# Causal attention in a two-layer block on one Trainium2 core: GpSimd inverts the row sums, VectorE masks four of the eight row blocks, and the order on all engines is new

## The chip, the cores and the metric

The kernel runs on one core of one Trainium2 chip. The metric is the device time of the program in microseconds (us): before, the median of three runs is 1507.27. The names in the profile are PE (TensorE, matrix products), PEld (its weight loads), DVE (VectorE), ACT (ScalarE), POOL (GpSimd) and SP (SyncE, which here issues all DMAs).

## The reference, cut to what matters

```python
# layer 0: x is (4, 1024, 128), 16 heads of 64
xn = layernorm(x)
qkv = einsum('bse,ehd->bshd', xn, qkv_w) + qkv_b
logits = einsum('bqhd,bkhd->bhqk', q, k) / sqrt(64)
logits = where(tril(ones(1024, 1024)), logits, large_negative)
probs = softmax(logits)
x = x + einsum('bhqk,bkhd->bqhd', probs, v) @ out_w + out_b + ffn(xn)   # ffn: silu(gate) * up
# layer 1, on the result: a delta-rule attention and a mixture of 8 experts; the change does not touch it
```

## The kernel before

Layer 0's attention is done in 32 units. Unit `u` is one batch (of 4) and one pair of heads (of 8). A unit has eight blocks of 128 query rows, called rows 0 to 7 here and in the code; row r sees keys 0 to 128(r+1). For each row and both heads:

1. TensorE makes the scores (L1022, `place_scores`) with q and k of 64 partitions for each head, so the two heads use one half each of the array's rows. Then it adds the triangular mask to the last 128 columns with one bf16 product for each head (L1024): identity times mask, accumulated on the scores.
2. VectorE takes the maximum, negated (`maximum`, L687). Rows 4 to 7 are done head by head, rows 0 to 3 both heads at once.
3. ScalarE takes the exponential (`softmax`, L528), which also gives the sum of the row, and writes into the buffer `big`.
4. VectorE takes the reciprocal of the row sums (`invert`, L697).
5. GpSimd multiplies the exponentials by it (`scale`, L447), head by head.
6. VectorE transposes 32 x 32 blocks in place (`turn`, L705).
7. When all rows of a group have been transposed, SP issues 16 DMAs (`move`, L354) that carry them from `big` to `across`, with the blocks exchanged between the partitions. Group 0 is rows 0, 1, 6, 7, group 1 is rows 2, 3, 4, 5.
8. One unit later TensorE multiplies them by the values (`weigh`, L1083), ScalarE copies the result (`keep_att`, L543), TensorE applies the output weights (`join`, L1107), ScalarE copies (`keep_join`) and GpSimd adds to `x1` (L459).

`big` has one place for each group. So the exponentials of a group in unit u+1 wait until its 16 DMAs of unit u have landed (the wait on `moved` in `softmax`), and so does `weigh` of unit u. The scores of rows 4 to 7 lie in `both`, those of rows 0 to 3 in `flips_all`, each with room for one row (rows 0 and 1 share), so the scores of the next row wait for the exponentials of the last.

Between these pieces, TensorE makes q, k and v of the next unit (`project`, L990; `project_values`, L1000), which ScalarE copies out (`keep_part`, `keep_values`). After each batch VectorE takes statistics of `x1` (`second_sums`, `second_variance` with L720), and one unit of the next batch has a `second_deviation` on GpSimd (L432 to L438). The order of every engine is written out by hand in its `unit(u)`; VectorE's `unit(u)` works on unit u-1. The `Tally` tables count semaphores in the same order.

Of the kernel before, what the change touches and what calls it, by code (L numbers as in the profile page):

```python
# [14 lines left out]
P = 128  # L15
# [74 lines left out]
TURNS = (5, 4)  # L90
SLOTS = [row for rows in STEP_ROWS for row in rows]
BANK = {('v', 0): 2, ('qk', 0, 1): 2, ('qk', 1, 0): 2, ('qk', 0, 0): 2, ('qk', 1, 1): 2, ('v', 1): 2, ('o', 0): 0, ('o', 1): 1}
# [30 lines left out]
EARLY = (('qk', 0, 1), ('qk', 1, 0))  # L123
# [39 lines left out]
def layer0(block, sem, sbuf, kept, early, shared, b2_sb, x, qkv_w, qkv_b, out_w, out_b, w_gate, w_up, w_down, ln_w, ln_b, w_slow, w_out, Wg, b1, late):  # L163
# [15 lines left out]
                ((7, 0), -1), ((7, 1), -1), ((0,), -1), ((1,), -1), ((6, 1), -1), ((6, 0), -1), ((2,), -1),  # L179
                ((5, 1), -1), ((5, 0), -1), ((3,), -1), ((4, 0), -1), ((4, 1), -1),  # L180
            ])
    exps_at = Tally([
                ((7, 0), 0), ((7, 1), 0), ((6, 1), 0), ((6, 0), 0), ((5, 1), 0), ((5, 0), 0), ((4, 0), 0),
                ((4, 1), 0),
# [8 lines left out]
                (('v', 0), 0), (('qk', 0, 1), 1), (('qk', 1, 0), 1), (('qk', 0, 0), 1), (('qk', 1, 1), 1),  # L193
                (('v', 1), 1),
# [5 lines left out]
                ((7, 1), 0), ((1, 1), 0), ((7, 0), 0), ((0, 0), 0), ((0, 1), 0), ((1, 0), 0), ((6, 0), 0),  # L200
                ((6, 1), 0), ((2, 0), 0), ((2, 1), 0), ((5, 0), 0), ((3, 0), 0), ((3, 1), 0), ((5, 1), 0),
# [3 lines left out]
                ((0,), -1), ((4,), -1), ((1,), -1), ((6,), -1), ((2,), -1), ((5,), -1), ((3,), -1),  # L205
# [7 lines left out]
    with ctx:  # L213
# [11 lines left out]
        recip = sb("recip", [P, 2, ROWS, 2])  # L225
        spare = sb("spare", [P, 1008])
# [22 lines left out]
        ident_made, mask_made, const_step, halves_made = sem("ident_made"), sem("mask_made"), sem("const_step"), sem("halves_made")  # L249
# [13 lines left out]
        recip_ready, scaled = sem("recip_ready"), sem("scaled")  # L263
        second_var, second_rstd, second_step, stats_step = sem("second_var"), sem("second_rstd"), sem("second_step"), sem("stats_step")
# [50 lines left out]
        def _(sp):  # L315
# [40 lines left out]
            for u in range(UNITS):  # L356
                if u == 2:
                    sp.wait_ge(xn_flipped, 2 * B)
                    sp.dma_start(w1_sb, W1.rearrange("x e h -> e x h")).then_inc(experts_loaded, 16)
                if u == UNITS - 1:  # L360
                    for c in range(2):
                        for half in range(2):
                            k, use = use_of(u, "qk", c, half)
                            sp.wait_ge(bank_made[k], use)
                    sp.dma_start(w2_sb, W2.rearrange("x (j p) e -> p x j e", p=P)).then_inc(experts_loaded, 16)
                    sp.wait_ge(b2_cleared, 1)
                    sp.dma_start(b2_sb[0:X, :], b2).then_inc(experts_loaded, 16)
                move(u, 0)
                move(u, 1)
# [3 lines left out]
        def _(pool):  # L373
# [47 lines left out]
            def constants():  # L421
# [5 lines left out]
                pool.memset(score[:], 0.0).then_inc(score_cleared, 1)  # L427

            def second_deviation(b):
# [9 lines left out]
                                   ALU.mult).then_inc(second_rstd, 1)  # L439

# [20 lines left out]
            def unit(u):  # L461
                scale(u, 7, 1)
                scale(u, 1, 1)
                scale(u, 7, 0)
                scale(u, 0, 0)
                scale(u, 0, 1)
                scale(u, 1, 0)
                scale(u, 6, 0)
                scale(u, 6, 1)
                scale(u, 2, 0)  # L470
                scale(u, 2, 1)
                if u > PAIRS and u % PAIRS == 2 and u < UNITS:
                    second_deviation(u // PAIRS - 1)
                scale(u, 5, 0)
                scale(u, 3, 0)
                scale(u, 3, 1)
                scale(u, 5, 1)
# [8 lines left out]
            tails["gpsimd"] = scale, add_part  # L486

        @block.scalar
        def _(act):
# [74 lines left out]
            def unit(u):  # L564
                if u == 0:
                    keep_values(0, 0)
# [4 lines left out]
                softmax(u, 0, 0)  # L571
                softmax(u, 0, 1)
                softmax(u, 1, 0)
                softmax(u, 1, 1)
                keep_part(u + 1, 0, 1)
                softmax(u, 6, 1)
                keep_part(u + 1, 1, 0)
                softmax(u, 6, 0)
                keep_att(u - 1, 0)
                keep_part(u + 1, 0, 0)  # L580
                softmax(u, 2, 1)
                softmax(u, 2, 0)
                softmax(u, 5, 1)
                softmax(u, 5, 0)
                softmax(u, 3, 1)
                softmax(u, 3, 0)
                keep_part(u + 1, 1, 1)
                keep_att(u - 1, 1)
                softmax(u, 4, 0)
                softmax(u, 4, 1)  # L590
                keep_values(u + 1, 1)
                keep_join(u - 1, 0)
                keep_join(u - 1, 1)
                keep_values(u + 1, 0)
# [58 lines left out]

# [5 lines left out]
        def _(dve):  # L659
# [13 lines left out]

            def maximum(u, row, *h):
# [4 lines left out]
                if step < SMALL:  # L679
                    dve.wait_ge(scores_ready, scores_at(u, step))  # L680
                else:
                    for k in h or range(2):
                        dve.wait_ge(bank_made[k], uses_at[k](u, "s", step))
# [4 lines left out]

            def invert(u, step):
                if done(u):  # L690
                    return
                recips_at.meet(u, step)
                for h in range(2):
                    dve.wait_ge(*exponents_of(u, step, h))
                lo = SLOTS.index(STEP_ROWS[step][0])
                part = slice(lo, lo + len(STEP_ROWS[step]))
                dve.reciprocal(recip[:, u % 2, part, :], row_sum[:, u % 2, part, :]).then_inc(recip_ready, 1)  # L697
# [33 lines left out]
            def unit(u):  # L731
                if u == 2:
                    constants()
                maximum(u - 1, 7, 0)
                maximum(u - 1, 7, 1)
                maximum(u - 1, 0)
                maximum(u - 1, 1)
                invert(u - 1, 0)
                invert(u - 1, 4)
# [6 lines left out]
                turn(u - 1, 7)  # L746
                turn(u - 1, 0)
                invert(u - 1, 1)
                maximum(u - 1, 2)
                turn(u - 1, 1)  # L750
                turn(u - 1, 6, 0)
                turn(u - 1, 6, 1)
                maximum(u - 1, 5, 1)
                invert(u - 1, 6)
                maximum(u - 1, 5, 0)
                if u == 1:
                    add_branch(B - 1, (1,))
                if batch_over(u - 3):
                    second_sums(u - 3, GROUPS[1])
                maximum(u - 1, 3)  # L760
                invert(u - 1, 2)
                turn(u - 1, 2)
                invert(u - 1, 5)
                maximum(u - 1, 4, 0)
                maximum(u - 1, 4, 1)
                if batch_over(u - 3):
                    second_variance(u - 3, GROUPS[0])
                turn(u - 1, 3)
                invert(u - 1, 3)
                turn(u - 1, 5)  # L770
                turn(u - 1, 4)
                if batch_over(u - 3):
# [88 lines left out]
            keep_part(0, 0, 1)  # L861
# [9 lines left out]
            keep_part(0, 1, 0)  # L871
# [5 lines left out]
            keep_part(0, 0, 0)  # L877
# [8 lines left out]
            tails["vector"] = maximum, invert, turn, second_sums, second_variance  # L886

        @block.tensor
        def _(pe):
# [124 lines left out]
            def place_scores(u, row):  # L1014

                q, k = qk_sb[:, u % 2, 0, :], qk_sb[:, u % 2, 1, :]
                lo, hi = place_of(row)
                for a in range(lo, hi, 512):
                    z = min(a + 512, hi)
                    for h in range(2):  # L1020
                        part = slice(D * h, D * (h + 1))
                        pe.matmul(scores_of(row, h)[:, a - lo:z - lo], lhsT=q[part, P * row:P * (row + 1)], rhs=k[part, a - lo:z - lo],  # L1022
                                  start=True, stop=z < hi)
# [87 lines left out]
            def unit(u):  # L1111
                if u == 0:
# [3 lines left out]
                project_values(u, 0)  # L1116
                score_small(u, 4)
                weigh(u - 1, 0, 0, 4)
# [3 lines left out]
                project(u + 1, 0, 1)  # L1122
                score_small(u, 6)
                project(u + 1, 1, 0)
                weigh(u - 1, 0, 4, 8)
                project(u + 1, 0, 0)
# [3 lines left out]
                project(u + 1, 1, 1)  # L1130
                score_small(u, 5)
                weigh(u - 1, 1, 0, 4)
                score(u, 3)
                weigh(u - 1, 1, 4, 6)
                project_values(u + 1, 1)
                join(u - 1, 0)
                join(u - 1, 1)
# [8 lines left out]
            project(0, 0, 1)  # L1146
# [8 lines left out]
            project(0, 1, 0)  # L1155
# [8 lines left out]
            project(0, 0, 0)  # L1164
# [7 lines left out]
            pe.wait_ge(v_loaded, 16)  # L1172
            project_values(0, 1)
            hidden(3, 2)

# [120 lines left out]
def layer1(block, sem, sbuf, kept, early, shared, ended, b2_sb, late, out):  # L1296
# [136 lines left out]
    with ctx:  # L1433
# [98 lines left out]
        def _(sp):  # L1532
            last_move = tails["sync"]
            for t in range(ROWS):
# [6 lines left out]
        def _(pool):  # L1541
# [80 lines left out]
            last_scale, last_add = tails["gpsimd"]  # L1622
# [573 lines left out]
        def _(dve):  # L2196
# [189 lines left out]
            last_maximum, last_invert, last_turn, last_sums, last_variance = tails["vector"]  # L2386
            last_maximum(UNITS - 1, 7, 0)
            last_maximum(UNITS - 1, 7, 1)
            last_maximum(UNITS - 1, 0)
            last_maximum(UNITS - 1, 1)  # L2390
            last_invert(UNITS - 1, 0)
            last_invert(UNITS - 1, 4)
            last_maximum(UNITS - 1, 6, 1)
            last_maximum(UNITS - 1, 6, 0)
            last_turn(UNITS - 1, 7)
            last_turn(UNITS - 1, 0)
            last_invert(UNITS - 1, 1)
            last_maximum(UNITS - 1, 2)
            last_turn(UNITS - 1, 1)
            last_turn(UNITS - 1, 6, 0)  # L2400
            last_turn(UNITS - 1, 6, 1)
            last_maximum(UNITS - 1, 5, 1)
            last_invert(UNITS - 1, 6)
# [876 lines left out]
```

## Time and profile before

| | |
|---|---|
| median of 3 runs | 1507.27 us (1505.23 to 1508.43) |
| profiled execution | 1510.43 us, with a span of 1508.7 us |
| mean TensorE clock granted | 0.99 of full speed |
| TensorE, VectorE, GpSimd, ScalarE busy | 97, 83, 64, 62% of the span |
| attention stage | about 95 to 957 us of the span |
| the chain that ended last | PE 62%, SP's DMA issues 13%, DVE 8%, DMA 5%, ACT 4% |

The shares are of the whole span, both layers together. The bulk of the time is a loop over the units with a constant pattern, so what a change of the loop is worth is read from one period and multiplied.

### The profile page before, as it was taken

The page shows a single profiled execution, that of the slowest core. Times are in us where ns is not written, and L with a number is a line of the kernel's source. Part 1 is how long each engine was busy: PE and PEld are TensorE (multiplying, and loading weights), DVE is VectorE, ACT ScalarE, POOL GpSimd, SP SyncE. Part 2 cuts the span into 40 slices and gives each one's busy share as a digit, 9 for nine tenths or more (in the row PEclk, how much of TensorE's full clock was granted, in tenths as well). Part 3 has the DMA queues.
Part 4 walks back from the last instruction along what each step waited for, and adds up shares of the span by engine and source line. Part 5 has one row for each costly group of instructions (what it writes and reads, how often), then busy time and mean ns, then how long its engine had stood idle before and what let it go on. Part 6 is the DMA issues. An engine that isn't in the chain of part 4 may idle for free.

```text
span 1508.7 us, 26195 instructions
## 1 busy us (share of the span) xinstructions
PE 1456.1 (97%) x8770; PEld 874.5 (58%) x8770; DVE 1252.7 (83%) x1966; ACT 928.3 (62%) x1862; POOL 967.3 (64%) x752
## 2 busy tenths in 40 slices
PE   8899999999999999999999999887999999999998
PEld 6645545555455455555554555454677676776767
DVE  7577787788777888877788778377999999999997
ACT  4356666666666666666666666444766676657562
POOL 5134555546545556455456554519999999999895
PEclk9989999999999999999999999998999999999999
DMA  8058777777777777778777778400000000000000
GB/s 186 1 126 200 169 169 180 179 163 174 180 169 174 168 181 173 166 172 184 167 171 169 184 173 191 107 1 1 1 8 7 1 8 1 8 8 1 8 1 15
DMA packets 77136, 163.91 MB, mean 109 GB/s; under 512 B 31410, under 2 KB 43724, under 8 KB 77004
## 3 DMA queue, kind: packets, MB, share of 16 engines
q1 hardware_dynamic: 77004, 162.24, 46.6%
q8 instruction: 72, 1.18, 0.3%
q14 instruction: 60, 0.49, 0.1%
HBM read 9.08 MB, written 2.10 MB: 7 GB/s over the span
## 4 chain that ended last, share of the span: by engine, by line
PE 62%; SPq 13%; DVE 8%; DMA 5%; issue 5%; ACT 4%; POOL 2%; DVEq 0%; ACTq 0%; POOLq 0%
SPq L354 13%; PE accum L1083 11%; PE both L2772 10%; PE both L1022 6%; PE flips_all L2795 5%; DVE big L705 5%; DMA across<-big 5%; PE flips_all L2784 4%; PE flips_all L1022 3%; ACT big L528 3%; PE flips_all L2832 3%; PE misc L990 2%; PE accum L2784 2%; PE accum L2795 2%; PE flips_all L2818 2%
## 5 line engine op out<-in xcount | busy, mean ns | idle before, releaser
L447 POOL TENSOR_SCALAR big<-big,recip 128x1024 f32<-128x1024 f32 (+7 forms) x512 | 374.4, 745 | 447.0 <-DVE recip L697 446.8
L705 DVE STREAM_TRANSPOSE big<-big 128x896 f32<-128x896 f32 (+7 forms) x288 | 345.5, 1226 | 4.7 <-POOL big L447 2.6
L687 DVE TENSOR_REDUCE neg_max<-both 128x1 f32<-128x1024 f32 (+3 forms) x256 | 249.7, 1007 | 73.8 <-PE both L1024 73.8
L1083 PE MATMUL accum<-across,v_sb 128*64 128x256 f32 (+1 forms) x2560 | 278.5, 364 | 0.0
L528 ACT ACTIVATE big<-both,neg_max 128x1024 f32<-128x1024 f32 (+3 forms) x256 | 242.8, 951 | 44.6 <-DVE neg_max L687 44.5
L1083 PEld LDWEIGHTS accum<-across,v_sb 128*64 128x64 f32 x2560 | 169.0, 137 | 100.0 <-issue 25.8
L1022 PE MATMUL both<-qk_sb 64*128 64x512 f32 (+3 forms) x1024 | 215.8, 540 | 5.7 <-ACT big L528 3.5
L2772 PE MATMUL both<-slow_sb,h_T 128*128 128x512 f32 x384 | 182.5, 602 | 10.8 <-DVE xnT L2285 7.2
L1581 POOL TENSOR_TENSOR prod<-xnT,qs 128x1024 f32<-128x1024 f32 (+3 forms) x32 | 180.1, 5636 | 0.0
L1022 PEld LDWEIGHTS both<-qk_sb 64*128 64x128 f32 x1024 | 89.0, 187 | 118.8 <-issue 115.1
L528 ACT ACTIVATE big<-flips_all,neg_max 128x128 f32<-128x128 f32 (+3 forms) x256 | 131.7, 525 | 41.0 <-DMA across<-big 29.0
L990 PE MATMUL misc<-xnT,w_qk 128*128 128x512 f32 x256 | 139.0, 625 | 0.8 <-ACT qk_sb L507 0.8
L507 ACT ACTIVATE qk_sb<-misc,columns 128x512 f32<-128x512 f32 x124 | 85.2, 687 | 78.2 <-PE misc L990 78.2
L2772 PEld LDWEIGHTS both<-slow_sb,h_T 128*128 128x128 f32 x384 | 70.4, 193 | 86.5 <-issue 68.4
L1022 PE MATMUL flips_all<-qk_sb 64*128 64x384 f32 (+3 forms) x512 | 103.7, 480 | 13.1 <-ACT big L528 12.7
L697 DVE RECIPROCAL recip<-row_sum 128x2 f32<-128x2 f32 (+1 forms) x224 | 36.4, 163 | 94.7 <-ACT big L528 94.7
L1573 POOL TENSOR_TENSOR prod<-xnT 128x1024 f32<-128x1024 f32 (+2 forms) x24 | 109.0, 4544 | 0.5 <-DVE misc L2319 0.3
L687 DVE TENSOR_REDUCE neg_max<-flips_all 128x2 f32<-128x256 f32 (+3 forms) x128 | 101.5, 812 | 5.0 <-PE flips_all L1024 4.4
L1619 POOL TENSOR_TENSOR terms<-terms 128x1024 f32<-128x1024 f32 x42 | 99.3, 2364 | 3.4 <-DVE terms L2373 1.4
L2795 PEld LDWEIGHTS flips_all<-w_qk,hid 128*128 128x128 f32 x736 | 87.0, 192 | 14.6 <-issue 9.4
L2325 DVE TENSOR_REDUCE misc<-prod 128x16 f32<-128x1024 f32 (+3 forms) x32 | 90.2, 2817 | 4.1 <-POOL prod L1581 4.0
L2795 PE MATMUL flips_all<-w_qk,hid 128*128 128x128 f32 x736 | 90.4, 276 | 1.3 <-ACT hid L1779 1.2
(223 smaller groups left out, 2381.2 us busy)
## 6 DMA issues: line engine op xcount, KB each, us to landing
across<-big SPq DMA_DIRECT2D x1024, 144.0 KB, 3.0
out<-x SPq DMA_DIRECT2D x8, 256.0 KB, 2.3
x<-in_L_attn_x SPq DMA_DIRECT2D x3, 512.0 KB, 5.7
slow_sb<-in_L_attn_w_slow SPq DMA_DIRECT2D x3, 512.0 KB, 7.7
w_qk<-in_L_attn_qkv_w SPq DMA_DIRECT2D x2, 512.0 KB, 6.4
xn<-in_L_ffn_W SPq DMA_DIRECT2D x1, 1024.0 KB
x<-in_L_attn_x SPq DMA_DIRECT2D x2, 256.0 KB, 2.9
qs<-in_L_attn_qkv_w SPq DMA_DIRECT2D x1, 512.0 KB, 6.1
```

Of the source, the lines that this page charges most:

```text
L354: sp.dma_start(across[g][32 * b:32 * (b + 1), a, :], runs[g][32 * a:32 * (a + 1), b, :]).then_inc(moved[g], 16)
L447: pool.tensor_scalar(part, part, recip[:, u % 2, SLOTS.index(row), h:h + 1], 0.0, ALU.mult, ALU.add).then_inc(scaled, 1)
L528: last = act.activation(probs_of(row, h).rearrange("p b j k -> p j b k"), scores_of(row, h).rearrange("p (j b k) -> p j b k", b=MOVES, k=3 ...
L687: dve.tensor_reduce(out=dst, in_=src, axis=AX.X, op=ALU.max, negate=True).then_inc(max_ready, 1)
L705: dve.transpose(part, part).then_inc(turned[group_of(row)], 1)
L990: pe.matmul(pool_of[k], lhsT=w_qk[:, c, P * n:P * (n + 1)], rhs=xnT[:, u // PAIRS, 512 * half:512 * (half + 1)], start=True, stop=True).th ...
L1022: pe.matmul(scores_of(row, h)[:, a - lo:z - lo], lhsT=q[part, P * row:P * (row + 1)], rhs=k[part, a - lo:z - lo], start=True, stop=z < hi)
L1083: last = pe.matmul(dst, lhsT=values_of(u, j, h), rhs=keys_of(g, rows[n:n + 2], j, h), start=j == 0, stop=j == rows[n + 1])
L1573: pool.tensor_tensor(prod[s % 2][:, 0:s, :], ks[:, 0:s, :], ks[:, s:s + 1, :].broadcast_to([P, s, HD]), ALU.mult).then_inc(prod_ready, 1)
L1581: pool.tensor_tensor(prod[s % 2][:, s:2 * s + 1, :], ks[:, 0:s + 1, :], qs[:, s % 2:s % 2 + 1, :].broadcast_to([P, s + 1, HD]), ALU.mult). ...
L2772: last = pe.matmul(places[k][:, 512 * half:512 * (half + 1)], lhsT=h_T[:, P * s:P * (s + 1)], rhs=slow_sb[:, c, 512 * half:512 * (half + 1 ...
L2795: last = pe.matmul(places[k][:, P * s:P * (s + 1)], lhsT=hid[:, e % 2, j, P * s:P * (s + 1)], rhs=w2_sb[:, e, j, :], start=j == 0, stop=j ...
```

## The change

GpSimd takes over `invert`: the row sums to the power minus one, as a two-tensor instruction with a constant tile `minus_one`. VectorE loses its reciprocals and gets `cover`, which adds the mask to the last 128 columns of the scores of rows 0 and 1 (together), 2 and 3, in PSUM, ahead of their maximum. TensorE loses the mask products of these four rows and keeps those of rows 4 to 7. Every engine has a new order.

```diff
+COVERED = (4, 5, 6)          # the steps of rows (0, 1), 3 and 2
...
+            def invert(u, step):     # gpsimd
+                if done(u):
+                    return
+                recips_at.meet(u, step)
+                for h in range(2):
+                    pool.wait_ge(*exponents_of(u, step, h))
+                lo = SLOTS.index(STEP_ROWS[step][0])
+                part = slice(lo, lo + len(STEP_ROWS[step]))
+                pool.tensor_tensor(recip[:, u % 2, part, :], row_sum[:, u % 2, part, :], minus_one[:, 0:len(STEP_ROWS[step]), :], ALU.pow).then_inc(recip_ready, 1)
...
+            def cover(u, step):      # vector
+                if done(u):
+                    return
+                covers_at.meet(u, step)
+                scored(u, step, range(2))
+                rows = STEP_ROWS[step]
+                if len(rows) == 1:
+                    lo, hi = place_of(rows[0])
+                    part, wide = (both if step < SMALL else flips_all)[:, :, hi - P:hi], mask.unsqueeze(1)
+                else:
+                    part = flips_all[:].rearrange("p h (r k) -> p h r k", r=2)[:, :, :, 0:P]
+                    wide = mask.unsqueeze(1).unsqueeze(1)
+                dve.tensor_tensor(part, part, wide.broadcast_to(part.shape), ALU.add).then_inc(covered, 1)
...
-                dve.reciprocal(recip[:, u % 2, part, :], row_sum[:, u % 2, part, :]).then_inc(recip_ready, 1)
...
             def unit(u):             # tensor
+                project(u + 1, 1, 0)
...
                 score(u, 0)
-                project_values(u, 0)
                 score_small(u, 4)
+                project_values(u + 1, 0)
...
             def place_scores(u, row):
...
+                if step_of(row) in COVERED:
+                    return last
                 return [pe.matmul(scores_of(row, h)[:, P * row:P * (row + 1)], lhsT=ident_half[:], rhs=mask_half[:],
                                   start=False, stop=True) for h in range(2)]
```

On TensorE, in the second half of a unit. Before, the rows are the scores of row 5, a projection, row 3, the weighing of group 1 (key blocks 0 to 3), row 4:

```order
L1022 MATMUL both<-qk_sb 128x512 x2
L1022 MATMUL both<-qk_sb 128x256 x2
L1024 MATMUL both<-mask_half,ident_half 128x128 x2
L990 MATMUL misc<-xnT,w_qk 128x512
L1022 MATMUL flips_all<-qk_sb 128x512 x2
L1024 MATMUL flips_all<-mask_half,ident_half 128x128 x2
L1083 MATMUL accum<-across,v_sb 64x4x64 x6
L1083 MATMUL accum<-across,v_sb 64x4x32 x2
L1083 MATMUL accum<-across,v_sb 64x4x64 x8
L1022 MATMUL both<-qk_sb 128x512 x2
L1022 MATMUL both<-qk_sb 128x128 x2
L1024 MATMUL both<-mask_half,ident_half 128x128 x2
```

And of the change, in the same place (its lines have other numbers; L1052 is the scores, L1056 the mask, L1115 the weighing):

```order
L1052 MATMUL both<-qk_sb 128x512 x2
L1052 MATMUL both<-qk_sb 128x256 x2
L1056 MATMUL both<-mask_half,ident_half 128x128 x2
L1029 MATMUL misc<-qs,xnT 128x256 x2
L1115 MATMUL accum<-across,v_sb 64x4x64 x6
L1115 MATMUL accum<-across,v_sb 64x4x32 x2
L1115 MATMUL accum<-across,v_sb 64x4x64 x8
L1052 MATMUL flips_all<-qk_sb 128x512 x2
L1115 MATMUL accum<-across,v_sb 64x4x64 x2
L1115 MATMUL accum<-across,v_sb 64x4x32 x2
L1052 MATMUL both<-qk_sb 128x512 x2
L1052 MATMUL both<-qk_sb 128x128 x2
```

The first weighing now stands in front of row 3's scores, and the second (key blocks 4 and 5) in front of row 4's.

On VectorE, from the maxima of row 5 to the end of the unit. Before:

```order
L687 TENSOR_REDUCE neg_max<-both 128x1
L697 RECIPROCAL recip<-row_sum 128x2
L687 TENSOR_REDUCE neg_max<-both 128x1
L687 TENSOR_REDUCE neg_max<-flips_all 128x2
L697 RECIPROCAL recip<-row_sum 128x2
L705 STREAM_TRANSPOSE big<-big 128x4x192
L697 RECIPROCAL recip<-row_sum 128x2
L687 TENSOR_REDUCE neg_max<-both 128x1 x2
L705 STREAM_TRANSPOSE big<-big 128x4x256
L697 RECIPROCAL recip<-row_sum 128x2
L705 STREAM_TRANSPOSE big<-big 128x4x384
L705 STREAM_TRANSPOSE big<-big 128x4x320
```

And of the change (L717 is the mask's addition):

```order
L730 TENSOR_REDUCE neg_max<-both 128x1 x2
L717 TENSOR_TENSOR flips_all<-flips_all,e_buf 128x2x128
L730 TENSOR_REDUCE neg_max<-flips_all 128x2
L730 TENSOR_REDUCE neg_max<-both 128x1 x2
L738 STREAM_TRANSPOSE big<-big 128x4x384
L738 STREAM_TRANSPOSE big<-big 128x4x192
L738 STREAM_TRANSPOSE big<-big 128x4x256
L738 STREAM_TRANSPOSE big<-big 128x4x320
```

The transposes of rows 5, 2, 3 and 4 now all stand behind the maxima of row 4; before, row 2's stood in front of them.

On GpSimd, the same part of the unit, in the change alone (before, these are the same scalings without L457, with row 3's two between row 5's):

```order
L457 TENSOR_TENSOR recip<-row_sum,minus_one 128x2
L465 TENSOR_SCALAR big<-big,recip 128x4x3x32 x2
L457 TENSOR_TENSOR recip<-row_sum,minus_one 128x2
L465 TENSOR_SCALAR big<-big,recip 128x4x6x32 x2
L457 TENSOR_TENSOR recip<-row_sum,minus_one 128x2
L465 TENSOR_SCALAR big<-big,recip 128x4x4x32 x2
L457 TENSOR_TENSOR recip<-row_sum,minus_one 128x2
L465 TENSOR_SCALAR big<-big,recip 128x4x5x32 x2
```

A power now stands in front of each row's two scalings.

## Rows read from the trace of the kernel before

**Rows 1.** Page, part 1: busy time of the engines and share of the span.
```profile
PE 1456.1 (97%) x8770; PEld 874.5 (58%) x8770; DVE 1252.7 (83%) x1966; ACT 928.3 (62%) x1862; POOL 967.3 (64%) x752
```

**Rows 2.** Chain that ended last, 395 to 423: start us, us, what.
```profile
395.12 0.80 PE accum L1083 x8
...
401.82 0.42 PE flips_all L1022 x4
...
402.45 0.63 PE flips_all L1022 x4
...
415.99 1.09 PE flips_all L1022 x4
417.08 0.22 PE flips_all L1024 x2
417.30 3.39 PE accum L1083 x32
420.69 1.28 PE both L1022 x8
...
422.19 0.82 PE accum L1083 x8
```

**Rows 3.** Timeline of VectorE, 414 to 429: start us, us, what [idle before].
```profile
413.97 2.06 DVE L705 STREAM_TRANSPOSE big<-big 128x896 f32<-128x896 f32 x2
...
422.23 1.55 DVE L687 TENSOR_REDUCE neg_max<-both 128x1 f32<-128x640 f32 x2 [1.62 <-PE both L1024]
423.70 1.24 DVE L705 STREAM_TRANSPOSE big<-big 128x1024 f32<-128x1024 f32 x1
425.38 0.17 DVE L697 RECIPROCAL recip<-row_sum 128x2 f32<-128x2 f32 x1 [0.44 <-ACT big L528]
425.48 3.35 DVE L705 STREAM_TRANSPOSE big<-big 128x1536 f32<-128x1536 f32 x2
```

**Rows 4.** Timeline of ScalarE, 402 to 425.
```profile
402.89 1.11 ACT L528 ACTIVATE big<-both,neg_max 128x1024 f32<-128x1024 f32 x1 [0.44 <-DVE neg_max L687]
...
414.62 0.58 ACT L528 ACTIVATE big<-flips_all,neg_max 128x384 f32<-128x384 f32 x1 [0.53 <-DMA across<-big]
...
423.62 0.79 ACT L528 ACTIVATE big<-both,neg_max 128x640 f32<-128x640 f32 x1
```

**Rows 5.** Timeline of GpSimd, 412 to 428.
```profile
412.65 2.00 POOL L447 TENSOR_SCALAR big<-big,recip 128x896 f32<-128x896 f32 x2 [2.72 <-DVE recip L697]
...
425.64 1.57 POOL L447 TENSOR_SCALAR big<-big,recip 128x640 f32<-128x640 f32 x2 [2.70 <-DVE recip L697]
```

**Rows 6.** Timeline of VectorE: last two transposes of units 1 and 30.
```profile
124.14 3.35 DVE L705 STREAM_TRANSPOSE big<-big 128x1536 f32<-128x1536 f32 x2
...
920.41 3.35 DVE L705 STREAM_TRANSPOSE big<-big 128x1536 f32<-128x1536 f32 x2
```

**Rows 7.** VectorE in 260 to 1040, shapes apart: busy us, mean ns.
```profile
L687 DVE TENSOR_REDUCE neg_max<-flips_all 128x2 f32<-128x1024 f32 x25 | 30.3, 1213 | 2.6 <-PE flips_all L1024 2.6
...
L2285 DVE SCALAR_TENSOR_TENSOR qs<-both,e_buf 128x1024 f32<-128x1024 f32 x4 | 4.9, 1222 | 5.6 <-ACT e_buf L1835 5.6
...
L720 DVE BATCH_NORM_AGGREGATE var<-stats 128x2 f32<-128x6 f32 x32 | 2.9, 152 | 0.1
```

**Rows 8.** GpSimd in 0 to 260, shapes apart.
```profile
L447 POOL TENSOR_SCALAR big<-big,recip 128x512 f32<-128x512 f32 x14 | 9.5, 692 | 4.8 <-DVE recip L697 4.8
...
L401 POOL TENSOR_TENSOR e_buf<-e_buf,minus_half 128x8 f32<-128x8 f32 x3 | 5.1, 1696 | 0.2
...
L394 POOL TENSOR_TENSOR e_buf<-e_buf,minus_half 128x4 f32<-128x4 f32 x2 | 2.0, 1014 | 0.2
```

**Rows 9.** Timeline of GpSimd, 582 to 593.
```profile
582.70 0.20 POOL L432 TENSOR_TENSOR rstd<-var,eps 128x8 f32<-128x8 f32 x1
...
586.79 3.13 POOL L447 TENSOR_SCALAR big<-big,recip 128x768 f32<-128x768 f32 x4
590.52 1.57 POOL L447 TENSOR_SCALAR big<-big,recip 128x640 f32<-128x640 f32 x2 [0.61 <-DVE recip L697]
```

More of the change, by code:

```diff
@@ L367, in _ @@
                     sp.dma_start(b2_sb[0:X, :], b2).then_inc(experts_loaded, 16)
+                move(u - 1, 1)
                 move(u, 0)
-                move(u, 1)
             tails["sync"] = move
@@ L652, in _ @@
             silu(3, 2)
+            keep_part(0, 0, 0)
             for u in range(UNITS):
@@ L678, in maximum @@
                 step = step_of(row)
[L679 to L683, printed above, removed]
+                scored(u, step, h or range(2))
+                if step in COVERED:
+                    dve.wait_ge(covered, covers_at(u, step))
                 src, dst = both_scores(row), neg_max[:, u % 2, row, :]
@@ L733, in unit @@
                     constants()
-                maximum(u - 1, 7, 0)
-                maximum(u - 1, 7, 1)
+                cover(u - 1, 4)
                 maximum(u - 1, 0)
                 maximum(u - 1, 1)
-                invert(u - 1, 0)
-                invert(u - 1, 4)
                 maximum(u - 1, 6, 1)
@@ L746, in unit @@
                 turn(u - 1, 7)
+                cover(u - 1, 6)
+                turn(u - 1, 1)
+                maximum(u - 1, 2)
                 turn(u - 1, 0)
-                invert(u - 1, 1)
-                maximum(u - 1, 2)
-                turn(u - 1, 1)
+                turn(u - 1, 6, 1)
                 turn(u - 1, 6, 0)
-                turn(u - 1, 6, 1)
+                maximum(u - 1, 5, 0)
                 maximum(u - 1, 5, 1)
-                invert(u - 1, 6)
-                maximum(u - 1, 5, 0)
                 if u == 1:
@@ L759, in unit @@
                     second_sums(u - 3, GROUPS[1])
+                cover(u - 1, 5)
                 maximum(u - 1, 3)
[L761 to L763 removed]
+                maximum(u - 1, 4, 1)
                 maximum(u - 1, 4, 0)
[L765 removed]
                 if batch_over(u - 3):
                     second_variance(u - 3, GROUPS[0])
+                turn(u - 1, 5)
+                turn(u - 1, 2)
                 turn(u - 1, 3)
[L769 to L770 removed]
                 turn(u - 1, 4)
+                maximum(u, 7, 0)
+                maximum(u, 7, 1)
                 if batch_over(u - 3):
@@ L885, in _ @@
                 unit(u)
-            tails["vector"] = maximum, invert, turn, second_sums, second_variance
+            tails["vector"] = cover, maximum, turn, second_sums, second_variance
         @block.tensor
@@ L1017, in place_scores @@
                 lo, hi = place_of(row)
+                last = [None, None]
                 for a in range(lo, hi, 512):
@@ L1021, in place_scores @@
                         part = slice(D * h, D * (h + 1))
-                        pe.matmul(scores_of(row, h)[:, a - lo:z - lo], lhsT=q[part, P * row:P * (row + 1)], rhs=k[part, a - lo:z - lo],
-                                  start=True, stop=z < hi)
+                        last[h] = pe.matmul(scores_of(row, h)[:, a - lo:z - lo], lhsT=q[part, P * row:P * (row + 1)], rhs=k[part, a - lo:z - lo],
+                                  start=True, stop=z < hi or step_of(row) in COVERED)
+                if step_of(row) in COVERED:
+                    return last
                 return [pe.matmul(scores_of(row, h)[:, P * row:P * (row + 1)], lhsT=ident_half[:], rhs=mask_half[:],
```

159 lines of the change are left out of this document (82 added, 77 removed).

## The prediction

> **What bounds the kernel now.** The page's first part [rows 1] shows TensorE 97% busy, VectorE 83%, GpSimd 64%. That suggests that work taken from TensorE is gained in full. The chain that ended last says otherwise: 13% of it are SP's DMA issues. So I looked for a loop that the moves close, and read the timelines of the unit at 402 to 429.
>
> The loop runs through group 1. Row 2's exponential starts at 414.62, and the idle time before it was ended by a DMA [rows 4]. The unit's last two transposes start at 425.48 and take 3.35, so they end at 428.83 [rows 3]: 14.21 later. Then SP issues the 16 DMAs of group 1, they land, and row 2's next exponential starts. One period is (920.41 - 124.14)/29 = 27.46 over units 1 to 30 [rows 6], so the move takes 27.46 - 14.21 = 13.25 on average. TensorE needs nearly as much: in the chain the weighing at 395.12 and the one at 422.19 are the same place of two units, 27.07 apart, with nothing but TensorE between them [rows 2]. The reader is to see two limits 0.4 apart: the move loop at 27.46, which rules, and TensorE at 27.07.
>
> **TensorE after the change.** A row's mask products take 0.22 [rows 2], so four rows give 0.88. There is more. The scores of row 0 (128 columns, 0.42) and row 1 (256 columns, 0.63) differ by 0.21 for 128 columns, so each carries 0.21 that does not depend on its columns [rows 2]: the price of coming from the full array to two halves. Row 1 now follows row 0, and row 5 follows row 2, directly: 0.42 less. Two products that stood behind a cheap mask product now come straight from the halves: I charge 0.15 each (bounds 0 and 0.21). TensorE's need falls to 27.07 - 0.88 - 0.42 + 0.3 = 26.07.
>
> **The move loop after the change**, counted from row 2's exponential as 0.
> - TensorE: weighing of group 1 starts at 0.14 (it waits for the same DMAs), 3.39, then row 3's scores 1.09 [rows 2]: 4.62. Weighing of blocks 4 and 5: 0.82 + 0.15. Row 4: 1.28 + 0.22 [rows 2]. Row 4 is ready at 7.1; before it was 422.19 - 414.62 = 7.57.
> - VectorE: its first maximum starts 0.04 later, 7.13. The two take 1.47 (422.23 to 423.70), row 3's transpose 1.16 (1.24 less the 0.08 that neighbours overlap), those of rows 5 and 4 3.35 together [rows 3], less 0.1 since they are apart. Row 2's is 0.9, by the line through 1.07 for 896 elements (half of 2.06, and overlap) and 1.24 for 1024 [rows 3]. The last would start at 7.13 + 1.47 + 1.7 + 0.9 + 1.16 = 12.4 and end at 13.9.
> - The power. No row has one of two elements. 128x4 takes 1.01 and 128x8 1.70 [rows 8], 0.17 an element; the line gives 0.67 for 128x2. Lower bound: the reciprocal's 0.17 [rows 3]; upper bound: 1.01. I take 0.67, since the line has its two ends near it.
> - The mask's addition. Two tensors, one in PSUM, 1024 elements: 1.22; the smallest VectorE row here 0.15 [rows 7]. 256 elements by the line: 0.42 (bounds 0.15 and 1.22). Row 3: ready 4.62, masked 5.08, maximum 1.21 [rows 7] to 6.36. That is before row 4 is ready, with 0.77 to spare, so VectorE's additions are hidden while they take less than 1.2. The two other additions stand where VectorE waits for row 6 and where it waits for the move.
> - GpSimd: row 3's exponentials follow at 6.38. Row 4's pair takes 1.76 with the hop to the next engine (423.62 to 425.38) [rows 3, 4]; 512 columns instead of 640 take 0.1 less each, so 7.93. Power 0.67; hop 0.07; two scalings of 0.69 [rows 8] less overlap, 1.35; power 0.67; hop 0.07; two scalings of row 4, 1.57 [rows 5]; hop 0.1. That makes 12.43, a hair behind VectorE's 12.4. Row 4's transpose 1.52 ends the loop at 13.95.
>
> So two things meet: TensorE delivers row 4 0.47 earlier; row 2's transpose, which now stands behind row 4's maxima, and the powers take that back but for 14.21 - 13.95 = 0.26. The period is 27.20, still the move loop's. TensorE, at 26.07, then waits over 1 us in each period.
>
> [...] By the rows the power costs four times the reciprocal (0.67 against 0.17). [...]
>
> **Terms that take back.**
> - In three units GpSimd computes the deviations, 582.70 to 586.79, 4.1 us [rows 9]. Before, this was hidden: GpSimd idled 0.61 in front of row 4's scalings [rows 9]. Now four powers are in the same queue. From row 2's exponentials at 1.2: 0.77, 0.6, 4.1, 0.6, 0.67, 1.8, 0.67, 1.35, 0.67, 0.07 + 1.57, 0.1 and 1.52 make 15.8, which is 1.85 over 13.95: 3 x 1.85 = 5.5.
> - In three units the four aggregates of 0.15 [rows 7] now stand between row 4's maxima and the transposes, in the loop: 3 x 0.5 = 1.5.
> - Group 0 has a loop too: from row 7's exponential, 402.89, to its last transpose, 413.97 + 2.06 = 416.03 [rows 3, 4], is 13.14; with the move 26.4. GpSimd there gets powers of 1.01 and 0.67 in front of scalings that ended 1.38 ahead of the last transpose (414.65 [rows 5]), about one transpose ahead, so with little slack. I expect 0.6 to 1.2 more: 27.0 to 27.6, around the new period. Moves vary, so part of this shows: 0.05 in 30 periods, 1.5.
> - The first unit has no move ahead of it and gains from TensorE: -0.5. Layer 1 keeps its instructions, and the chain that leads into it is the same.
>
> **Sum.** 30 x -0.26 + 5.5 + 1.5 + 1.5 - 0.5 = +0.2. On the profiled execution's 1510.4 that is 1510.6; on the median, 3.1 below it, 1507.5. Each 0.1 us in the loop is 3 us.
>
> **The rivals.**
> - The full gain of TensorE. 27.46 to 26.07 in 31 units, 43 us less or 1464. For it: TensorE 97% busy. Against: row 2's exponential is released by a DMA [rows 4], and what the loop computes between two moves, 13.95, is fixed by waits in which TensorE's gain is only partly contained. Chance 0.05.
> - A shorter loop. Power under 0.6 (VectorE's 13.9 rules), deviations cost 1 us a unit, group 0 nothing: 30 x -0.31 + 3 + 1.5 - 0.5 = -5, so 1502; with TensorE's products closer, down to 1496. Chance 0.32.
> - The power as the bound. With power p the loop ends at 12.61 + 2p; from p = 0.73 on it is over 14.07, at which the other terms make it slower than before by the bound below. At 0.85 it ends at 14.31: +3 and the 8 us of the other terms and 1.5 for the deviations, 1520; at 1.01, 14.63, 1531. For it: the smallest power in the trace is 1.01. Chance 0.2.
> - Group 0's loop rules, at 27.6: 30 x 0.14 + 5.5 + 1.5 - 0.5 = +11, 1518. It decides from 1.0 us more between row 7's exponential and the last transpose of group 0. Chance 0.13.
> - My forecast, no change within 0.2%: 0.3.
>
> **How the numbers follow.** A measurement of this kernel can tell about 0.2% (3 us) from no change. Faster: 0.05 + 0.32 = 0.37. Same: 0.3. Slower: 0.2 + 0.13 = 0.33. Both signs hold much, so the forecast's own range is 1504.5 to 1510.5, and the range for 8 in 10 reaches from 1496 to 1521: it leaves out the full gain and the dearest powers.
>
> **What would show it.** In the profile after: TensorE's share falls by 2 to 4 points with a wait in front of the weighing of group 1; row 2's exponential still released by a DMA; 13.9 to 14.0 from it to the end of row 4's transpose; powers of 0.67; additions of 0.42 to 0.5; the period 27.2; units with deviations over 1 us longer. The prediction is wrong if row 2's exponential waits for no DMA any more, if the powers are far from 0.67, or if GpSimd is what row 6's transposes wait for in every unit.

## The result and the profile after

The changed kernel takes 1514.69 us (median of 10 runs, 1512.58 to 1519.84) against 1507.27 for the kernel before (median of 10 as well): ratio 1.005 (95% interval 1.0038 to 1.0061). It is slower by 0.5%, inside the range and on its upper side, not the 1507.5 forecast. The profiled execution took 1519.84, the slowest of the ten, and has a span of 1518.1, 9.4 over the 1508.7 before. Below, the 9.4 are divided by loop and unit; they are differences of two single executions.

The page's first part answers [rows 1]:

```profile
PE 1428.7 (94%) x8514; PEld 876.2 (58%) x8514; DVE 1273.0 (84%) x1838; ACT 921.1 (61%) x1862; POOL 1132.8 (75%) x977
```

TensorE does 27 us less and 256 matmuls less, and the kernel is longer. GpSimd does 166 us more, which is what its powers take: six of 0.70 and one of 1.01 in each of 32 units, 167.

The ordinary unit. These are the changed kernel's timelines of ScalarE, of VectorE and of GpSimd in one unit (start us, us, what, idle before and releaser); they answer [rows 3, 4, 5].

```profile
393.39 0.58 ACT L553 ACTIVATE big<-flips_all,neg_max 128x384 f32<-128x384 f32 x1 [2.03 <-DMA across<-big]
...
399.89 0.69 ACT L553 ACTIVATE big<-flips_all,neg_max 128x512 f32<-128x512 f32 x1 [0.43 <-DVE neg_max L730]
```

```profile
398.06 0.43 DVE L717 TENSOR_TENSOR flips_all<-flips_all,e_buf 128x256 f32<-128x256 f32 x1 [1.32 <-PE flips_all L1052]
398.63 1.22 DVE L730 TENSOR_REDUCE neg_max<-flips_all 128x2 f32<-128x1024 f32 x1
400.25 1.55 DVE L730 TENSOR_REDUCE neg_max<-both 128x1 f32<-128x640 f32 x2 [0.40 <-PE both L1056]
401.73 3.75 DVE L738 STREAM_TRANSPOSE big<-big 128x1536 f32<-128x1536 f32 x3
406.09 1.51 DVE L738 STREAM_TRANSPOSE big<-big 128x1280 f32<-128x1280 f32 x1 [0.61 <-POOL big L465]
```

```profile
398.73 1.79 POOL L465 TENSOR_SCALAR big<-big,recip 128x768 f32<-128x768 f32 x2
401.48 0.70 POOL L457 TENSOR_TENSOR recip<-row_sum,minus_one 128x2 f32<-128x2 f32 x1 [0.96 <-ACT big L553]
402.28 1.37 POOL L465 TENSOR_SCALAR big<-big,recip 128x512 f32<-128x512 f32 x2
403.61 0.70 POOL L457 TENSOR_TENSOR recip<-row_sum,minus_one 128x2 f32<-128x2 f32 x1
404.41 1.58 POOL L465 TENSOR_SCALAR big<-big,recip 128x640 f32<-128x640 f32 x2
```

Row 2's exponential is still released by a DMA. From its start to the end of row 4's transpose it is 406.09 + 1.51 - 393.39 = 14.21, the same as before, and 14.19 to 14.21 in all but eight units. The other three transposes are done at 401.73 + 3.75 = 405.48, and the last waits 0.61 for GpSimd. So GpSimd ends the loop, not VectorE: mask addition, maximum, exponentials, two powers and four scalings follow each other.

A period is counted here from the end of one unit's row 4 transpose to the next. What varies in it is the move, from that end to the next row 2 exponential: it takes 12.82 to 14.21 behind units 2 to 29 (12.80 to 14.11 before). SP starts its 16 issues 0.03 after the transpose and needs 10.1 to 11.6 for them, most of them 0.64 apart. So most of the move is the issuing of 16 DMAs; no experiment here changed it.

Two things are not ordinary. In unit 2 the chain that ended last (start us, us, what) reads:

```profile
136.98 0.92 PE misc L1029 x4
137.90 4.46 issue
142.36 6.08 PE accum L1115 x32
```

TensorE idles 4.46, then the 32 products of the first weighing, 3.39 in [rows 2], take 6.08. The reason for the idle stands on ScalarE:

```profile
142.35 0.58 ACT L553 ACTIVATE big<-flips_all,neg_max 128x384 f32<-128x384 f32 x1 [6.13 <-DMA across<-big]
```

And in the order of SP's queue. Here are the kernel before and the changed kernel, in the same stretch:

```profile
104.71 33.41 SPq L354 DMA_DIRECT2D across<-big  x38
138.16 0.58 SPq L359 DMA_DIRECT2D xn<-in_L_ffn_W  x1
141.80 3.71 SPq L354 DMA_DIRECT2D across<-big  x6
```

```profile
104.74 18.73 SPq L360 DMA_DIRECT2D across<-big  x20
123.51 0.68 SPq L365 DMA_DIRECT2D xn<-in_L_ffn_W  x1
125.40 20.11 SPq L360 DMA_DIRECT2D across<-big  x25
```

The new order of SP issues layer 1's 1 MB of W1 between the moves of group 0 and group 1 of unit 1; before, it stood behind group 1's move. Group 1 of unit 1 then moves in 17.0 us instead of 13.5. The table of busy times (length, each engine's busy us, TensorE's clock as a share of full, DMA share, GB/s) shows why the weighing is then slow:

```profile
120.00:137.00 17.00, 17.00 (x103) 8.72 (x102) 14.34 (x15) 11.28 (x26) 12.56 (x17) 1.00 0.99 237
137.00:142.30 5.30, 0.90 (x4) 0.44 (x3) 4.60 (x6) 0.00 (x0) 1.74 (x2) 0.87 0.69 163
142.30:148.50 6.20, 6.14 (x34) 3.95 (x36) 0.00 (x0) 3.49 (x9) 4.30 (x6) 0.56 0.91 218
148.50:157.00 8.50, 8.00 (x46) 4.49 (x48) 6.83 (x7) 5.93 (x13) 3.75 (x6) 1.00 0.42 87
```

The clock granted is 0.56 while the weighing runs, so most of it ran at the 1.2 GHz level, after 4.46 of idleness; it is 1.00 from 148.5 on. Unit 2's period is 33.80 against 27.67 before: +6.1 of the 9.4, in one unit.

The other thing is the unit with deviations. GpSimd of the changed kernel, unit 10:

```profile
366.65 0.59 POOL L465 TENSOR_SCALAR big<-big,recip 128x384 f32<-128x384 f32 x1
367.20 0.20 POOL L440 TENSOR_TENSOR rstd<-var,eps 128x8 f32<-128x8 f32 x1
...
371.29 0.59 POOL L465 TENSOR_SCALAR big<-big,recip 128x384 f32<-128x384 f32 x1
...
377.32 1.58 POOL L465 TENSOR_SCALAR big<-big,recip 128x640 f32<-128x640 f32 x2
```

The deviations stand between row 2's two scalings and delay all that follows. The loop of these three units (10, 18 and 26) is 16.04 or 16.05; before, it was 14.51, 14.55 and 14.20, so 4.9 are added. Six units (these and the one ahead of each) take 171.20 against 164.51: +6.7. The units ahead have loops of 14.20 and are 2.1 longer for longer moves.

The rest: first unit -1.2, unit 1 -0.9, the other 22 periods of 3 to 30 together -1.25; together with the two above 6.1 + 6.7 - 1.2 - 0.9 - 1.25 = 9.45. The last unit's period is 31.20 instead of 28.94, +2.3, which what follows it gives back.

### The profile page after: what moved, and what is told of

Same layout as the page of the kernel before. It is cut to its first block, busy times and chain, and to the rows that moved or that the text cites. A ratio compares the mean times of both kernels' runs of the same rounds, so it can differ in the third digit from the quotient of the medians.

```text
span 1518.1 us, 25876 instructions
## 1 busy us (share of the span) xinstructions
PE 1428.7 (94%) x8514; PEld 876.2 (58%) x8514; DVE 1273.0 (84%) x1838; ACT 921.1 (61%) x1862; POOL 1132.8 (75%) x977
## 4 chain that ended last, share of the span: by engine, by line
PE 76%; DVE 8%; issue 6%; POOL 5%; ACT 2%; SPq 2%; DMA 1%; DVEq 0%; ACTq 0%; POOLq 0%
PE accum L1115 14%; PE both L2799 10%; PE both L1052 9%; PE misc L1019 7%; PE flips_all L1052 5%; PE flips_all L2822 5%; PE flips_all L2811 4%; PE misc L1029 3%; PE flips_all L1139 3%; DVE neg_max L730 3%; PE flips_all L2859 3%; PE accum L2811 2%; POOL big L465 2%; PE accum L2822 2%; SPq L360 2%
## 5 line engine op out<-in xcount | busy, mean ns | idle before, releaser
L465 POOL TENSOR_SCALAR big<-big,recip 128x384 f32<-128x384 f32 (+7 forms) x512 | 375.9, 749 | 22.1
L457 POOL TENSOR_TENSOR recip<-row_sum,minus_one 128x2 f32<-128x2 f32 (+1 forms) x224 | 166.7, 744 | 270.6 <-ACT big L553 270.6
L1115 PE MATMUL accum<-across,v_sb 128*64 128x256 f32 (+1 forms) x2560 | 282.3, 368 | 27.9 <-issue 27.9
L1115 PEld LDWEIGHTS accum<-across,v_sb 128*64 128x64 f32 x2560 | 182.4, 139 | 154.5 <-issue 95.8
L1052 PE MATMUL both<-qk_sb 64*128 64x512 f32 (+3 forms) x1024 | 211.1, 530 | 11.1 <-ACT big L553 10.6
L1052 PEld LDWEIGHTS both<-qk_sb 64*128 64x128 f32 x1024 | 93.4, 187 | 123.2 <-issue 123.1
L717 DVE TENSOR_TENSOR flips_all<-flips_all,e_buf 128x256 f32<-128x256 f32 (+1 forms) x96 | 49.5, 516 | 66.9 <-PE flips_all L1052 66.9
L1052 PE MATMUL flips_all<-qk_sb 64*128 64x384 f32 (+3 forms) x512 | 95.1, 469 | 0.0
```

The source lines that it names most:

```text
L457: pool.tensor_tensor(recip[:, u % 2, part, :], row_sum[:, u % 2, part, :], minus_one[:, 0:len(STEP_ROWS[step]), :], ALU.pow).then_inc(reci ...
L465: pool.tensor_scalar(part, part, recip[:, u % 2, SLOTS.index(row), h:h + 1], 0.0, ALU.mult, ALU.add).then_inc(scaled, 1)
L1052: last[h] = pe.matmul(scores_of(row, h)[:, a - lo:z - lo], lhsT=q[part, P * row:P * (row + 1)], rhs=k[part, a - lo:z - lo], start=True, st ...
L1115: last = pe.matmul(dst, lhsT=values_of(u, j, h), rhs=keys_of(g, rows[n:n + 2], j, h), start=j == 0, stop=j == rows[n + 1])
```

## The experiments

Four theories, in the letters of the expectations: A, W1's load ahead of a move costs some 5 us; C, the deviations between row 2's scalings cost some 5; E, GpSimd's powers end the ordinary loop and take back what TensorE lost; H, the power alone costs what the loop's arithmetic gives for it. All ratios are to the kernel before on the same chip (medians 1508.06 to 1508.28), with the 95% interval. Between the kernel before of the result, 1507.27, and these lies 0.8 to 1.0; a difference of two medians is uncertain by that much at least.

**W1's load back behind the move, in the changed kernel.**

```diff
-                if u == 2: (wait, W1's dma_start)
                 move(u - 1, 1)
+                if u == 2: (wait, W1's dma_start)
```

> The changed kernel with one edit: the 1 MB load of W1 is issued behind the 16 DMAs of group 1 of unit 1, where the kernel before has it, and not in front of them. Theory A (the load's place costs some 6 us: row 2's exponential of unit 2 waits 4.1 us longer than usual, TensorE idles and then runs one weighing at 0.56 of its clock): 1507.5 to 1509, period of unit 2 back from 33.8 to about 27.5. Rival B (unit 2 is slow because the new order needs a unit to settle): 1514 to 1515.5, no change.

1510.89, ratio 1.002 (1.0007 to 1.0033); the changed kernel had 1.005. Unit 2's period is 28.40 and its loop 14.19. The chain shows what is left:

```profile
138.87 1.69 issue
140.56 3.46 PE accum L1115 x32
```

After an idle of 1.69 the weighing keeps its 3.46. The time is above A's range and far from B's. A's mechanism holds, its price was too high: 33.80 - 28.40 = 5.4 in unit 2 of the profiles, 3.8 between the medians (4.8, if each is taken against its own kernel before). The profile of the change shows a dear case: in the four other traces of the experiments with the load in the same place and SP's new order, unit 2 takes 30.89 to 31.87.

**The same load between the moves, in the kernel before.**

> The kernel before with one edit: the load of W1 is issued between the DMAs of group 0 and of group 1 of unit 1, as in the changed kernel. Theory A: 1510 to 1514, a period of some 33 at unit 2 and a clock near half in its first weighing. Rival B: 1506.5 to 1508, no change.

1511.47, 1.002 (1.0007 to 1.0032). Unit 2's period is 31.57 and its weighing takes 5.03:

```profile
144.60 1.13 PE flips_all L1022 x4
145.73 0.22 PE flips_all L1024 x2
145.94 5.03 PE accum L1083 x32
```

The clock granted is 0.68 in that weighing. One line moved on SP costs some 3 us in a kernel with nothing else changed. A holds from the other side; the price is smaller here than the 3.8 (1514.69 - 1510.89) there, by less than these runs tell apart.

**Deviations behind row 4's scalings, in the changed kernel.**

```diff
-                if u > PAIRS and ...: second_deviation(u // PAIRS - 1)
                 scale(u, 4, 0)
                 scale(u, 4, 1)
+                if u > PAIRS and ...: second_deviation(u // PAIRS - 1)
```

> The changed kernel with one edit: the deviations of the second norm (4.1 us on GpSimd in three units) stand behind the scalings of row 4, not between those of row 2. Theory C (in the GpSimd queue of the new kernel they push row 4's scalings and so the last transpose): 1509 to 1511, periods of units 10, 18, 26 from 29.0 to about 27.3. Rival D (these units are long because of VectorE's statistics and aggregates, which are in them or next to them): 1513.5 to 1515.

1512.03, 1.0027 (1.0015 to 1.004). The three units' loops are 14.20 or 14.21. GpSimd of this run, unit 10:

```profile
372.05 1.58 POOL L465 TENSOR_SCALAR big<-big,recip 128x640 f32<-128x640 f32 x2
373.60 0.20 POOL L440 TENSOR_TENSOR rstd<-var,eps 128x8 f32<-128x8 f32 x1
...
377.66 2.51 POOL L477 TENSOR_TENSOR x<-o_buf,x 128x512 f32<-128x512 f32 x2
380.12 0.71 POOL L457 TENSOR_TENSOR recip<-row_sum,minus_one 128x2 f32<-128x2 f32 x1
```

The additions to `x1` behind them take the delay, and the loop no longer waits for it. The time lies between the ranges of C and D. C holds for the loop: in the profiles the periods of the three units fall from 87.1 to 82.3, by 4.8. In the medians 2.7 of the change's time came back (3.7 against their own kernels before), less than the 5.5 charged.

**A copy in place of the power, in the changed kernel.**

```diff
-                pool.tensor_tensor(recip[...], row_sum[...], minus_one[...], ALU.pow)
+                pool.tensor_copy(recip[...], row_sum[...])
```

> The changed kernel with GpSimd's power replaced by a copy of the row sums, so the probabilities are multiplied by the sums and not divided: it leaves out the reciprocals. Theory E (the two powers in front of row 3's and row 4's scalings hold the last transpose): the loop from row 2's exponential to the last transpose goes from 14.21 to about 13.9, ordinary periods to 26.8, units with deviations save over 1 us more: 1500 to 1505. Rival F (VectorE's transposes, all four behind row 4's maxima, hold it as well): 1511 to 1514, the loop still over 14.1.

1497.17, 0.9916 (0.9895 to 0.9936), below what was expected. The copy takes 0.19, and the loop 13.48 to 13.77 in ordinary units. Now GpSimd is early and VectorE has no gap; TensorE rules. Its chain in this run:

```profile
386.58 1.11 PE flips_all L1052 x4
...
387.78 0.44 DVE flips_all L717
...
388.35 1.24 DVE neg_max L730
...
390.19 0.20 ACT big L553
...
390.44 1.16 PE flips_all L1139 x8
...
413.17 1.11 PE flips_all L1052 x4
```

Row 3's scores start 413.17 - 386.58 = 26.59 apart. In that period TensorE waits once, about 0.5: `join` (L1139) writes into `flips_all`, which row 3's first exponential reads until 390.39. So 26.1 is TensorE's own need, and 26.6 the floor that the new order has. E holds, and its prize is 15.5 in the 22 ordinary periods against the changed kernel, 0.7 each.

**The power alone, in the kernel before**: its reciprocals replaced by powers on GpSimd, each in front of its scalings; masks and order as before.

> The kernel before with the first part of the change alone: GpSimd takes the row sums to the power minus one in front of each row's scalings, VectorE has no reciprocals, all else and its order as before. Theory H (the power is longer than the reciprocal and stands in the move loop): row 4's exponentials end 10.7 after row 2's start; 0.1, power 0.70, 0.1, scalings 1.57, 0.1, transpose 1.52 end the loop at 14.75 and not 14.21, so 0.54 in some 30 periods: 1520 to 1526. Rival G (the reciprocals' place on VectorE was the wait, so the power alone is no loss): 1505 to 1511.

1527.03, 1.0128 (1.0112 to 1.0144). The loop is 14.78 (before 14.21), 15.93 where there are deviations. Row 4's last steps, GpSimd's timeline and then VectorE's:

```profile
405.17 0.70 POOL L453 TENSOR_TENSOR recip<-row_sum,minus_one 128x2 f32<-128x2 f32 x1 [1.83 <-ACT big L549]
405.96 1.57 POOL L461 TENSOR_SCALAR big<-big,recip 128x640 f32<-128x640 f32 x2
```

```profile
407.64 1.51 DVE L716 STREAM_TRANSPOSE big<-big 128x1280 f32<-128x1280 f32 x1 [1.30 <-POOL big L461]
```

0.57 in 30 units is 17, and +18.9 was measured, 1 above H's range. H holds for the loop, but that the sum comes so near is partly luck: of the 16.3 by which the profiled span is longer, the 22 ordinary periods are only 8.3 (0.38 each, not 0.57), and the six with and ahead of the deviations 6.7, which the sum did not have.

**The mask on VectorE alone, in the kernel before**: `cover` ahead of the maxima of rows (0, 1), 2 and 3, reciprocals and order as before.

> The kernel before with the second part alone: VectorE adds the mask of rows 0 to 3 ahead of their maxima, TensorE has no mask products for them, all else and its order as before. Theory H: TensorE's need falls to about 26.3 but the move loop stays at 14.1 to 14.2, since row 4's scores come only some 0.1 earlier: 1503 to 1508. Rival I (VectorE, with 1.55 us more in each unit, becomes late in the loop): 1512 to 1522. Rival J (TensorE ruled after all): under 1495.

1505.26, 0.9984 (0.9971 to 0.9996): -2.8. The loop is 13.99 instead of 14.21, since row 3's mask products are gone from in front of row 4's scores. The loops of the units with deviations go the other way: 14.92 to 15.39, where the kernel before had 14.20 to 14.55. That takes part of it back.

**Row 2's transpose in front of row 3's mask addition, in the changed kernel.**

```diff
+                turn(u - 1, 2)
                 cover(u - 1, 5)
...
                 turn(u - 1, 5)
-                turn(u - 1, 2)
```

> The changed kernel with row 2's transpose put back in front of the mask addition and the maximum of row 3, so that only three transposes stand behind row 4's maxima. Theory E (GpSimd with its two powers holds the last transpose): the loop stays at 14.20 and the time at 1513 to 1517. Rival F (the transposes behind row 4's maxima hold it): the loop falls by up to 0.9, 1495 to 1508.

1525.46 (1517.54 to 1528.45), 1.0109 (1.0086 to 1.0131). The ordinary loop is 14.18 or 14.19: unchanged, as E has it, for the transpose was not what ended it. But in a unit with deviations VectorE of this run waits with row 2's transpose for them, and row 3's addition and maximum stand behind it:

```profile
368.45 0.98 DVE L738 STREAM_TRANSPOSE big<-big 128x768 f32<-128x768 f32 x1 [4.13 <-POOL big L465]
```

These loops are 17.88. It is slower than either theory had. The profile is of the shortest execution, 1517.54; the other five take up to 11 more, and what they lose is in no trace, so that part stays open.

**Row 4's inversion back on VectorE, in the changed kernel**, as a reciprocal behind row 5's transpose; the other rows keep their powers.

```diff
                 turn(u - 1, 5)
+                invert_fourth(u - 1)     # dve.reciprocal for row 4
                 turn(u - 1, 2)
...
-                invert(u, 3)             # gpsimd
```

> The changed kernel with row 4's inversion back on VectorE, as a reciprocal behind row 5's transpose; the other rows keep the power on GpSimd. Theory E: row 4's scalings follow row 3's directly, the last transpose ends 0.7 earlier on GpSimd's side and VectorE's side rules at 13.5 to 13.8: loop 13.65 to 13.85, periods of some 26.8, 1500 to 1506. Rival F (VectorE gives no room): the loop over 14.1, 1512 or more.

1501.62, 0.9953 (0.9939 to 0.9967). GpSimd of this run scales rows 3 and 4 without a pause, and VectorE of it has no gap ahead of the last transposes:

```profile
395.89 0.70 POOL L457 TENSOR_TENSOR recip<-row_sum,minus_one 128x2 f32<-128x2 f32 x1 [2.15 <-ACT big L555]
396.69 2.94 POOL L468 TENSOR_SCALAR big<-big,recip 128x512 f32<-128x512 f32 x4
```

```profile
396.14 1.77 DVE L748 STREAM_TRANSPOSE big<-big 128x1536 f32<-128x1536 f32 x1
397.83 0.12 DVE L740 RECIPROCAL recip<-row_sum 128x2 f32<-128x2 f32 x1
397.88 3.47 DVE L748 STREAM_TRANSPOSE big<-big 128x768 f32<-128x768 f32 x3
```

The ordinary loop is 13.54 to 13.83, as E has it. One of a unit's seven powers taken away gives back 13 us (1514.69 to 1501.62) for 0.12 on VectorE, which had waited there. This decides for E: the ordinary loop of the changed kernel is GpSimd's.

**The first and third edit together** (load back, deviations late).

> The changed kernel with two edits, both tried alone: the load of W1 behind group 1's DMAs, the deviations behind row 4's scalings. Theory: the two losses stand in different units and add, 4.9 + 3.8: 1505 to 1508, that is no difference from the kernel before, with every ordinary loop still at 14.2. Rival K (they overlap, and something else holds the rest): 1509 to 1512.

1508.8, 1.0002 (0.9988 to 1.0016), 0.8 above the theory's range and 0.2 under K's. By the ratios the two losses add: of the 7.4, all but 0.7 is gone, and no difference from the kernel before can be told.

**Those and the reciprocal of row 4.**

> As the last, and row 4's inversion on VectorE as well. Theory: the loop at 13.5 to 13.7, near TensorE's own need (26.6 with its wait), so 1491 to 1496, faster than both kernels. Rival K: over 1499.

1490.56, 0.9886 (0.9873 to 0.9899): 17.5 us faster than the kernel before on this chip (1508.06). The ordinary loop is 13.54 to 13.81.

**That with row 2's transpose moved as well.**

> As the last, and row 2's transpose in front of row 3's mask addition. Theory: GpSimd holds the loop in most units and VectorE in few, so up to 3 less than the last: 1489 to 1495. Rival L (the transpose placed early waits for row 2's scalings and delays row 3's maximum): the same or up to 3 more.

1491.78, 0.9896 (0.9883 to 0.9909): no difference. Of 31 periods 14 are 26.58 to 26.62, the floor found with the copy; the last one is 30.86.

**That with W2's load of unit 30 behind the group 1 move too.**

> As the last, and the load of W2 (1 MB, for layer 1) behind group 1's DMAs of unit 30, not in front of them. Theory (a megabyte in front of a move costs twice, in the wait and in TensorE's clock after it): 2 to 4 less than the last, and the last period down from 30 or more. Rival M (at unit 30 the load is over before the transposes end): no difference.

1489.22, 0.9881 (0.9864 to 0.9898). The last unit's period falls from 30.86 to 26.52 and the move ahead of it from 15.7 to 13.1. But the load's place does not decide alone: W2 stands in front too in the experiment with the deviations alone and in that with row 2's transpose alone, and their last periods are only 28.10 and 27.78. The intervals of the last three kernels overlap, and this run's profiled span is 1492.5, above the 1490.1 without the edit, so whether the 4.3 reach the end stays open.

## Why the prediction came out as it did

**The forecast "no change" was wrong by 7 us.** The range held, and so did the ruling loop, the move's. The range held partly by luck: the largest loss in the profile is one that no term had, and two terms that were charged, 1.5 each, did not come. Term by term, on the profiled spans:

- **A step that was missing.** "Layer 1 keeps its instructions, and the chain that leads into it is the same": it is not. SP's order changed as well, and W1's load came ahead of a move. Unit 2 is 6.1 longer in the profile, of which the load's place is 5.4, and 3.8 in the medians; the first two experiments show it from both sides. The sum had looked at the order of TensorE, VectorE and GpSimd only.
- **"30 x -0.26" was mis-sized.** The 22 ordinary periods give -1.25 in all, -0.06 each. The GpSimd side was put at 12.43 and VectorE's at 12.4. GpSimd's is 406.09 - 393.39 = 12.70: row 3's exponential starts at 6.50 instead of 6.38 (the maximum starts 0.14 after the addition), the power takes 0.70 instead of 0.67, and the two hops from power to scaling 0.10 each instead of 0.07. VectorE's is 405.48 - 393.39 = 12.09. So the loop was 14.21 instead of 13.95. The move was right: taken as 13.25, it is 13.2 on average in ordinary units. The bounds of the power held.
- **Deviations, "3 x 1.85 = 5.5": right in size.** The loop is 16.05, 1.84 over 14.21, though the terms written down end at 15.69 and not at 15.8. "Before, this was hidden" was not quite so: two of the three units had loops of 14.51 and 14.55 before, so 4.9 were added. Placing them late brought 2.7 to 3.7 back in the medians; why not more stays open.
- **Aggregates, 1.5: wrong.** Loops of the units with them (9, 17 and 25) are 14.20. VectorE had 0.61 to spare in front of row 4's transpose; in these units it has 0.34, so the aggregates fit in.
- **Group 0's loop, 1.5: not seen.** SP starts group 1's issues 0.03 after the transpose in units 1 to 29, so group 0's DMAs do not hold them up, and row 2's exponential waits for a DMA in every ordinary unit.
- **TensorE's need, 26.07: right.** The copy's periods of 26.58 hold a wait of 0.5. Its price list (0.22 for a mask, 0.21 to come back to two halves) is confirmed as a sum, not piece by piece. The rival "full gain" could not come even with free powers: `join` waits for row 3's exponentials, 0.5 in each unit, which the forecast did not have.
- **The mask addition, 0.42: right** (0.43), and hidden everywhere but in row 3, where it is on GpSimd's chain.
- **The rival "power as the bound"** had the right mechanism and the wrong price: from 12.61 + 2p one expects 14.01 at p = 0.70, and 14.21 came, for the later start and the hops above.
- **The signs of being wrong** did not show, and TensorE's share fell by 3 points, as forecast. Row 2's exponential waits for a DMA, the powers took 0.70, and VectorE waited for GpSimd with a transpose of row 6 in unit 0 only (0.23).

The power took 0.70 against 0.12 to 0.17 for VectorE's reciprocal, four times and more. The Trainium skill, GPSIMD Engine Reference, section "Performance versus the Vector engine", has an addition with two inputs and 2048 elements take 1.96 times as long on GpSimd as on VectorE. This case does not follow that factor for a power of two elements against a reciprocal; the measurement decides. For the same two elements a GpSimd copy took 0.19. So it is the power that is dear, not the engine.

**Where TensorE's gain went.** The change is +7.4. From the experiments, the powers are +18.9 (the deviations' loss stands in it as well, since the loops with deviations are 15.93 there), the masks -2.8 and W1's place +3.8. What the new order gives by itself is what remains, 7.4 - 18.9 + 2.8 - 3.8 = -12.5, or -13.5 with 4.8 for W1. It is worked out, not measured: no kernel had the new order alone, and the sum takes the powers' price from the old order.

## What to carry to other kernels

When a table of orders is new, compare every engine's queue, SP's above all: one load of 1 MB issued ahead of a move that closes a loop cost 3.5 us in the move, and then the clock. Before work is handed to an idle engine, add up the chain that it joins: GpSimd was 64% busy and idled 2.70 in front of its last scalings [rows 5], but two powers of 0.70 came to stand in series in the chain that ends the loop. And when the loop ends on one engine, try to give back the single instruction nearest its end: one reciprocal of 0.12 was worth 13 us.

## What the hardware showed that was not expected

- A weighing of 32 products took 3.46 after an idle of 1.69, and 6.08 at a granted clock of 0.56 after an idle of 4.46. The length of the idle does not decide alone. With the deviations late and nothing else edited, the last unit's weighing took 3.46 at a clock of 1.00, after an idle of 2.94. In the last experiment but one it took 5.14 at 0.67, after only 2.31. In the changed kernel it took 6.38 at 0.53, after 3.11. These are the three stretches, in this order:

```profile
937.60:941.30 3.70, 3.59 (x34) 2.72 (x36) 1.97 (x3) 3.00 (x8) 2.12 (x4) 1.00 0.53 122
920.40:925.60 5.20, 5.15 (x34) 3.69 (x34) 3.52 (x4) 3.11 (x8) 3.22 (x5) 0.67 0.47 107
947.20:953.70 6.50, 6.40 (x34) 4.04 (x34) 1.78 (x3) 3.00 (x8) 4.30 (x6) 0.53 0.67 151
```

- GpSimd's power took 0.70 for 128x2, 1.01 for 128x4 and 2.92 for 128x16 (L444, to the power minus one half, in the units with deviations): 0.16 for each further element, (2.92 - 0.70)/14, on some 0.4.
